# Attention in a transformer layer: row tile 0 is read and exponentiated behind tile 3, and ScalarE mixes row tile 2's far blocks ahead of q's evacuation

## The chip, the cores and the metric

The kernel runs on one core of a Trainium2 chip. The metric is device time in microseconds (us) of one execution, lower is better. Engines are named as in the profile: PE is the matrix engine (TensorE), DVE is VectorE, ACT is ScalarE, POOL is GpSimd, SP is the engine that issues most DMAs.

## The reference, cut to what matters

The input x is (8, 512, 512) in float32; there are 16 heads of 128. The layer is x + attention(layernorm(x)), then a routed feed-forward part on the result that the change does not touch. The attention mixes three softmaxes over the same scores:

```python
q = _rope((x @ Wq).reshape(b, n, H, HD)); k = _rope((x @ Wk).reshape(b, n, H, HD)); v = (x @ Wv).reshape(b, n, H, HD)
p_cmp = softmax over the 8 block means of k (blocks of 64 that lie fully in the past)
imp = p_cmp + 2.0 * cur_blk; sel = top_k(imp, 8)        # there are 8 blocks, so all are selected
p_slc = softmax(where(slc_mask, s_full, -1e30))         # the causal row
p_swa = softmax(where(causal & (i - j <= 64), s_full, -1e30))   # the window of 64
o = o_cmp * g_cmp + o_slc * g_slc + o_swa * g_swa
return o.reshape(b, n, H * HD) @ Wo
```

## The kernel before, in words

Matrix products are made of three passes over split operands (`hi` and `lo` parts), so each product needs a `hi` copy (ACT) and a `lo` difference (POOL or DVE) of its operands.

The attention is a software pipeline over 128 units. A unit is one head of one batch. In iteration u the engines work on three units at once: q, k and values of unit u are projected, unit u-1 is scored, and unit u-2 (in the code's numbering for the parts called `end`) has its probabilities transposed and multiplied with the values. A unit's 512 query rows are four row tiles t of 128 rows; tile t has its scores in PSUM bank t, and because of causality only the first (t+1)*128 columns count. Bank 0 has room left beside the 128 columns of tile 0, and there `sc` lies (the compressed branch's block sums of all four tiles, L428).

Nothing schedules this at run time: each engine has its own in-order program, written out by hand in a function `body` per engine, and semaphores tie them together.

- **PE** (L668): projects q and then k (24 matmuls, L650), scores the four tiles in the order 0, 3, 2, 1 (12 matmuls, L693), transposes the probabilities (10, L707), projects the values (24, L663), multiplies with the values (12, L728). The scores wait for `lo_done` of q and k from POOL, and tile by tile for `probs_ready` from DVE.
- **ACT** (L812): in one iteration it copies the finished output (`output_out`, L795), evacuates q from PSUM (`evacuate(u, 0)`, L764), mixes the far blocks of tiles 2 and 1 into `probs` (`mix_far`, L801: three instructions for tile 2, one for tile 1), copies the values (L809), evacuates k (L764 again), makes the `hi` parts of the transposed probabilities (L776), and then the exponentials of the rows (L782) and windows (L788) of tile 3, the `hi` copy of q (L771), the exponentials of tiles 2 and 1, the compressed branch's exponential (L843), the exponentials of tile 0, and the `hi` copy of k (L771). In the iterations that prepare the next pair of heads' weights, and in the last pair with those of Wo, it also makes weight copies (L152, L156, L1088), mostly behind the `hi` copy of k.
- **SP** (L524): stores the output, then moves the two halves of the evacuated q (later k) across partitions into `s_swap` (L501, L502), as the rotation of rope needs.
- **POOL** (L610): for q and then k three operations of rope each (L600, L601, L604), then the two `lo` parts (L608). The first waits for the evacuation and for the swap's landing.
- **DVE** (L936): causal mask (L897) of tiles 3 and 0; `read` of tile 3, which is the row minimum (L888), the window's minimum (L890) and the block sums into `sc` (L892); the `lo` parts of the transposed probabilities (L902); the mask of tiles 2 and 1; `read` of tiles 2, 1 and 0; the compressed branch (L954 to L960), which waits at L966 for ACT's exponentials; the coefficients, with `cmp_step` 7 at L972; then the mixes (L910, L926), of which the near part of tile 2 waits for ACT's far part (L985).

`masked_at` gives each tile's place in the list `MASKED`, the order of DVE's reads, and ACT's exponentials wait by it (L780, L787). ACT's evacuation of q waits for PE's projection of q and for POOL's `lo` of the q before it, since both use `s_full`:

```python
act.wait_ge(projected[k], u + 1)
act.wait_ge(lo_done[k], u)
nc.scalar.activation(s_full[k][:], banks[QK_BANK[k]][:, :], ACT.Copy, ...).then_inc(evacuated[k], 1)
```

Of the kernel before, what the change touches and what calls it, by code (L numbers as in the profile page):

```python
# [17 lines left out]
T = N // P  # L18
# [378 lines left out]
def attend(nc, phase, banks, m, gates, gates_full, xt_hi, xt_lo, weights, rope_d, misc_d, o_dram, gates_dram, chunks):  # L397
# [46 lines left out]
    cmp_step, exp_cmp, exp_row, exp_win = S("cmp_step"), S("exp_cmp"), S("exp_row"), S("exp_win")  # L444
# [13 lines left out]
    def pt_bank(u, g):  # L458

        if isinstance(u, int) and u >= U:  # L460
            return banks[((6, 5, 7), (0, 1, 2))[u - U][g]]
        return banks[(6, 5, 4)[g]]

    def out_bank(u):

        return banks[0 if isinstance(u, int) and u == U + 1 else 6]

    SCORED = [0, 3, 2, 1]
    MASKED = [3, 2, 1, 0]
    MIXED = [0, 3, 2, 1]  # L470
    scored_at = {t: i + 1 for i, t in enumerate(SCORED)}
    masked_at = {t: i + 1 for i, t in enumerate(MASKED)}
    mixed_at = {t: i + 1 for i, t in enumerate(MIXED)}
# [3 lines left out]
    def near(t):  # L477

        lo = WIN if t == 0 else 0
        return lo, t * P - WIN + lo, (t + 1) * P  # L480
# [277 lines left out]
    def scalar(act):  # L758
        def evacuate(u, k):

            act.wait_ge(projected[k], u + 1)
            if not (isinstance(u, int) and u == 0):
                act.wait_ge(lo_done[k], u)
            nc.scalar.activation(s_full[k][:], banks[QK_BANK[k]][:, :], ACT.Copy, scale=(-HD ** -0.5 if k == 0 else 1.0))\  # L764
                .then_inc(evacuated[k], 1)

        def high(u, k):
            act.wait_ge(roped[k], u + 1)
            if not (isinstance(u, int) and u == 0):
                act.wait_ge(scores_ready, u * T)  # L770
            nc.scalar.activation(qk_hi[k][:], s_full[k][:], ACT.Copy).then_inc(hi_done[k], 1)  # L771

        def pt_high(u, g):
            w = (512, 384, 384)[g]
            act.wait_ge(pt_ready, (u - 2) * 3 + g + 1)
            nc.scalar.activation(pt_hi[:, PTOFF[g]:PTOFF[g] + w], pt_bank(u, g)[:, 0:w], ACT.Copy).then_inc(pt_hi_done, 1)  # L776

        def exp_of_row(u, t):

            act.wait_ge(row_read, (u - 1) * T + masked_at[t])  # L780
            n = banks[t][:, 0:(t + 1) * P]
            nc.scalar.activation(n, n, ACT.Exp, bias=shift1[:, t:t + 1], scale=-1.0,  # L782
                                 accum_out=sums[:, 1, t:t + 1]).then_inc(exp_row, 1)

        def exp_of_window(u, t):
            lo = near(t)[0]
            act.wait_ge(win_masked, (u - 1) * T + masked_at[t])  # L787
            nc.scalar.activation(win[:, t, lo:], win[:, t, lo:], ACT.Exp, bias=shift2[:, t:t + 1], scale=-1.0,  # L788
                                 accum_out=sums[:, 2, t:t + 1]).then_inc(exp_win, 1)

        def output_out(u):

            act.wait_ge(out_ready, u - 2)
            act.wait_ge(out_slot_free, (u - 3) * 16 + 16)
            nc.scalar.activation(o_sb[:], out_bank(u - 1)[:, :], ACT.Copy).then_inc(out_evacuated, 1)  # L795

        def mix_far(v, t):

            act.wait_ge(cmp_step, v * NC + 7)
            for b in range(near(t)[1] // BS):  # L800
                last = nc.scalar.activation(probs[:, E1OFF[t] + b * BS:E1OFF[t] + (b + 1) * BS], banks[t][:, b * BS:(b + 1) * BS],  # L801
                                            ACT.Identity, scale=coef[:, 1, t:t + 1], bias=cb[:, t, b:b + 1])
            last.then_inc(far_mixed, 1)

        def values_high(u, j):

            act.wait_ge(projected[2], u)
            a, b = value_slots((j - 1) % 4)
            nc.scalar.activation(v_hi[:, a:b + 1:b - a].rearrange("p a i d -> p a (i d)"),  # L809
                                 banks[7][:, :].rearrange("p (a n) -> p a n", a=2), ACT.Copy).then_inc(v_hi_done, 1)  # L810

        def body(p, k, j, project=True, score=True, end=True, values=True, output=True, split=False, first=False):  # L812
            u = unit(p, k, j)
            if output:
                output_out(u)
            if project:
                evacuate(u, 0)
            if end:
                mix_far(u - 2, 2)
                mix_far(u - 2, 1)  # L820
            if values:
                values_high(u, j)
            if project:
                evacuate(u, 1)
            if first is not False:
                chunks.high_first(act, first)
            if end:
                for g in range(3):
                    pt_high(u, g)
            if score:  # L830
                exp_of_row(u, 3)
                exp_of_window(u, 3)
            if project:
                high(u, 0)
            if split is not False:
                weights.high(act, split, 0, j % 2)
            if score:
                exp_of_row(u, 2)
                exp_of_window(u, 2)
                exp_of_row(u, 1)  # L840
                exp_of_window(u, 1)
                act.wait_ge(cmp_step, (u - 1) * NC + 3)
                nc.scalar.activation(sc, sc, ACT.Exp).then_inc(exp_cmp, 1)  # L843
                exp_of_row(u, 0)
                exp_of_window(u, 0)
            if project:
                high(u, 1)
            if split is not False:
                if j % 2:
                    act.wait_ge(projected[2], split * PAIR)  # L850
                    weights.high_v(act, split)
                weights.high(act, split, 1, j % 2)

        def quad(p, k, split=False, wo=(), o=False):
            for j in range(4):
                body(p, k, j, split=split if j >= 2 else False)
                if j in wo:
                    chunks.high_wo(act, wo[j])
                if o and j < 2:
                    chunks.high_half(act, 2 * j)  # L860

        nc.scalar.activation(gates_full[:], gates_full[:], ACT.Sigmoid).then_inc(gates_squashed, 1)
        body(0, 0, 0, score=False, end=False, values=False, output=False)
        body(0, 0, 1, end=False, output=False)
        act.wait_ge(gates_stored, 16)
        body(0, 0, 2, output=False)
        body(0, 0, 3)
        for k in range(1, 3):
            quad(0, k)
        for p in range(1, PAIRS):  # L870
            quad(p - 1, 3, split=p)
            for k in range(0, 3):
                quad(p, k, wo=({}, {0: 0, 1: 1, 2: 2, 3: 3}, {0: 4, 1: 5, 2: 6, 3: 7})[k] if p == PAIRS - 1 else {})
        quad(PAIRS - 1, 3, wo={2: 8, 3: 9}, o=True)
        body(PAIRS, 0, 0, project=False, first=1)
        for n in range(10, H):
            chunks.high_wo(act, n)
        body(PAIRS, 0, 1, project=False, score=False, values=False, first=2)
        output_out(U + 2)
        chunks.high_first(act, 3)  # L880

    def vector(dve):
        def read(v, t):

            nb = 2 * (t + 1)
            n = banks[t]
            dve.wait_ge(causal_masked, v * T + MASKED_AT[t])
            nc.vector.tensor_reduce(shift1[:, t:t + 1], n[:, 0:(t + 1) * P], AX.X, ALU.min)  # L888
            lo, k0, k1 = near(t)
            nc.vector.tensor_tensor_reduce(out=win[:, t, lo:], in0=n[:, k0:k1], in1=m("window")[:, lo:], scale=1.0, scalar=3e38,  # L890
                                           op0=ALU.add, op1=ALU.min, accum_out=shift2[:, t:t + 1]).then_inc(win_masked, 1)
            nc.vector.reduce_sum(sc[:, t, 0:nb], n[:, 0:nb * BS].rearrange("p (n s) -> p n s", s=BS), AX.X).then_inc(row_read, 1)  # L892

        def mask(v, t):
# [19 lines left out]
        def mix_far(t):  # L914
            if t:
                k0 = near(t)[1]
                mix(t, (0, k0 // BS), probs[:, E1OFF[t]:E1OFF[t] + k0])
# [18 lines left out]
        def body(p, k, j, project=True, score=True, end=True, split=False):  # L936
            u = unit(p, k, j)
            v = u - 1
            gate = gates[:, bass.ds(k * 4 + j, 1)].rearrange("p o (r t) -> p (o r) t", t=T)
            if score:  # L940

                mask(v, 3)
                mask(v, 0)
                read(v, 3)
            if end:
                for g in range(3):
                    pt_low(u, g)
            if score:
                mask(v, 2)
                mask(v, 1)  # L950
                for t in (2, 1, 0):
                    read(v, t)
                dve.wait_ge(row_read, v * T + T)
                nc.vector.scalar_tensor_tensor(out=sc, in0=sc, scalar=-1.0 / BS,  # L954
# [820 lines left out]
```

## Time and profile before

| what | value |
|---|---|
| median of 3 runs | 2373.87 us (2372.65 to 2376.27) |
| the profiled execution's own time | 2379.06 us |
| its span, first to last instruction | 2377.1 us |
| mean granted TensorE clock | 0.994 of full speed |
| PE busy | 2309.4 us, 97% of the span |
| PE weight loads busy | 2031.2 us, 85% |
| DVE busy | 1844.1 us, 78% |
| POOL busy | 1633.4 us, 69% |
| ACT busy | 1489.1 us, 63% |

Busy time is a share of the whole span, which has several stages; the attention takes it from about 70 us to about 1800 us. The chain that ended last is PE for 66% of the span, DVE 11%, POOL 9%, ACT 5%, DMA 3%.

### The profile page before, as it was taken

What the parts mean: (1) busy time and instruction counts of PE and PEld (TensorE: products, weight loads), DVE (VectorE), ACT (ScalarE), POOL (GpSimd) and SP (SyncE); (2) the same over time, 40 slices, a digit from 0 to 9 for tenths busy, and PEclk for the clock granted to TensorE, in tenths of its full rate; (3) what the DMA queues carried; (4) which work ended last, traced back from release to release, by engine and by line L of the source; (5) the groups of instructions that cost most, each with busy time, mean ns of one, the idle gap of its engine ahead of it and who ended that gap; (6) DMA issues with size and microseconds to landing.
All of it is one profiled execution on the core that took longest, in us unless ns stands there. A gap on an engine that the chain in (4) does not pass through costs nothing.

```text
span 2377.1 us, 42098 instructions
## 1 busy us (share of the span) xinstructions
PE 2309.4 (97%) x13200; PEld 2031.2 (85%) x13200; DVE 1844.1 (78%) x6091; ACT 1489.1 (63%) x4174; POOL 1633.4 (69%) x1273
## 2 busy tenths in 40 slices
PE   6899999999999999999999999999998999998998
PEld 5799899988988998999899898888887788886787
DVE  8589898988988898898989898888884665566511
ACT  6577777777777777777777777777773111113343
POOL 2677877787777778777877877787883444444554
PEclk9999999999999999999999999999999999999999
DMA  5222222222222222222222222223333444453332
GB/s 173 74 58 64 73 76 54 72 78 63 59 72 78 54 67 82 64 58 76 74 63 59 73 76 54 71 83 93 85 89 123 167 170 153 152 196 105 110 117 80
DMA packets 143601, 213.34 MB, mean 90 GB/s; under 512 B 15008, under 2 KB 53280, under 8 KB 143392
## 3 DMA queue, kind: packets, MB, share of 16 engines
q1 hardware_dynamic: 137248, 196.17, 28.1%
q10 hardware_dynamic: 4224, 8.39, 0.9%
q0 software_dynamic: 1920, 6.24, 0.8%
q8 instruction: 101, 1.65, 0.3%
q14 instruction: 108, 0.88, 0.1%
HBM read 90.47 MB, written 53.22 MB: 60 GB/s over the span
## 4 chain that ended last, share of the span: by engine, by line
PE 66%; DVE 11%; POOL 9%; ACT 5%; DMA 3%; issue 2%; SPq 0%; POOLq 0%; ACTq 0%; DVEq 0%
PE bank L650 19%; PE bank L1132 13%; PE bank L663 10%; PE bank L693 7%; PE bank L728 7%; PE bank L707 4%; DMA s_swap<-s_full 3%; PE bank L1693 3%; PE bank L1674 3%; POOL s_full L600 3%; POOL s_swap L601 3%; POOL s_full L604 3%; DVE bank L892 1%; DVE pt_lo L902 1%; DVE shift L888 1%
## 5 line engine op out<-in xcount | busy, mean ns | idle before, releaser
L600 POOL TENSOR_TENSOR s_full<-s_full,rope 128x512 f32<-128x512 f32 x256 | 334.2, 1305 | 328.6 <-DMA s_swap<-s_full 328.3
L604 POOL TENSOR_TENSOR s_full<-s_full,s_swap 128x512 f32<-128x512 f32 x256 | 330.9, 1292 | 37.6 <-POOL s_swap L601 0.9
L601 POOL TENSOR_TENSOR s_swap<-s_swap,rope 128x512 f32<-128x512 f32 x256 | 330.9, 1293 | 0.0
L608 POOL TENSOR_TENSOR qk_lo<-s_full,qk_hi 128x512 fp32r<-128x512 f32 x256 | 326.3, 1294 | 0.0
L776 ACT ACTIVATE pt_hi<-bank 128x384 fp32r<-128x384 f32 (+1 forms) x384 | 174.4, 528 | 226.1 <-PE bank L707 226.1
L663 PE MATMUL bank<-wv_hi,xt_hi 128*128 128x256 f32 x1024 | 300.3, 293 | 0.0
L782 ACT ACTIVATE bank<-bank,shift 128x512 f32<-128x512 f32 (+3 forms) x512 | 257.1, 502 | 57.7 <-DVE bank L892 57.4
L663 PE MATMUL bank<-wv_hi,xt_lo 128*128 128x256 f32 x1024 | 290.0, 283 | 0.0
L663 PE MATMUL bank<-wv_lo,xt_hi 128*128 128x256 f32 x1024 | 289.9, 283 | 0.0
L1113 POOL TENSOR_TENSOR o_lo<-o_raw,o_hi 128x2048 fp32r<-128x2048 f32 x31 | 144.3, 4654 | 212.0 <-ACT o_hi L1292 185.5
L892 DVE TENSOR_REDUCE bank<-bank 128x8 f32<-128x512 f32 (+3 forms) x512 | 253.1, 494 | 0.0
L888 DVE TENSOR_REDUCE shift<-bank 128x1 f32<-128x512 f32 (+3 forms) x512 | 246.2, 481 | 0.0
L910 DVE SCALAR_TENSOR_TENSOR bank<-bank,coef,cb 128x192 f32<-128x192 f32 (+1 forms) x512 | 195.4, 405 | 55.0 <-ACT probs L801 55.0
L788 ACT ACTIVATE win<-win,shift 128x192 f32<-128x192 f32 (+1 forms) x512 | 225.6, 441 | 0.0
L771 ACT ACTIVATE qk_hi<-s_full 128x512 fp32r<-128x512 f32 x256 | 161.4, 630 | 91.1 <-POOL s_full L604 86.9
L902 DVE TENSOR_TENSOR pt_lo<-bank,pt_hi 128x384 fp32r<-128x384 f32 (+1 forms) x384 | 206.9, 594 | 8.4 <-ACT pt_hi L776 8.4
L650 PE MATMUL bank<-xt_hi,wq_hi 128*128 128x512 f32 x512 | 207.9, 406 | 0.8 <-PEq L201 0.8
L1132 PE MATMUL bank<-wo_hi,o_hi 128*128 128x512 f32 x512 | 205.2, 401 | 1.7 <-ACT s_swap L795 1.6
L650 PE MATMUL bank<-xt_hi,wq_lo 128*128 128x512 f32 x512 | 200.4, 391 | 0.0
L1132 PE MATMUL bank<-wo_hi,o_lo 128*128 128x512 f32 x512 | 200.4, 391 | 0.0
L1132 PE MATMUL bank<-wo_lo,o_hi 128*128 128x512 f32 x512 | 200.0, 391 | 0.0
L650 PE MATMUL bank<-xt_hi,wk_hi 128*128 128x512 f32 x512 | 199.2, 389 | 0.0
(190 smaller groups left out, 6899.1 us busy)
## 6 DMA issues: line engine op xcount, KB each, us to landing
s_swap<-s_full SPq DMA_DIRECT2D x512, 128.0 KB, 2.3
o_scratch<-s_swap SPq DMA_DIRECT2D x128, 256.0 KB, 2.0
o_raw<-o_scratch SPq DMA_DIRECT2D x32, 1024.0 KB, 5.4
w_raw<-in_L_ffn_W SPq DMA_DIRECT2D x64, 256.0 KB, 2.9
xin<-in_L_attn_x SPq DMA_DIRECT2D x14, 1024.0 KB, 5.5
z_scratch<-z ACTq DMA_DIRECT2D x8, 1024.0 KB, 4.3
out<-x SPq DMA_DIRECT2D x32, 256.0 KB, 2.1
wq_raw<-in_L_attn_Wq SPq DMA_DIRECT2D x16, 256.0 KB, 3.0
```

The costliest lines, as they stand in the source:

```text
L600: nc.gpsimd.tensor_tensor(s_full[k][:], s_full[k][:], rope[:, 0, :], ALU.mult).then_inc(cos_done[k], 1)
L601: nc.gpsimd.tensor_tensor(s_swap[k][:], s_swap[k][:], rope[:, 1, :], ALU.mult).then_inc(sin_done[k], 1)
L604: nc.gpsimd.tensor_tensor(s_full[k][:], s_full[k][:], s_swap[k][:], ALU.add).then_inc(roped[k], 1)
L608: nc.gpsimd.tensor_tensor(qk_lo[k][:], s_full[k][:], f32(qk_hi[k][:]), ALU.subtract).then_inc(lo_done[k], 1)
L650: last = nc.tensor.matmul(banks[QK_BANK[k]][:, :], w[k][s][:, c, :], v[:, b, c, :], start=(n == 0), stop=(n == 3 * C - 1))
L663: last = nc.tensor.matmul(out, x[:, b, c, at:at + P], w[:, c, :], start=(n == 0), stop=(n == 3 * C - 1), skip_group_check=True)
L782: nc.scalar.activation(n, n, ACT.Exp, bias=shift1[:, t:t + 1], scale=-1.0, accum_out=sums[:, 1, t:t + 1]).then_inc(exp_row, 1)
L788: nc.scalar.activation(win[:, t, lo:], win[:, t, lo:], ACT.Exp, bias=shift2[:, t:t + 1], scale=-1.0, accum_out=sums[:, 2, t:t + 1]).then_i ...
L888: nc.vector.tensor_reduce(shift1[:, t:t + 1], n[:, 0:(t + 1) * P], AX.X, ALU.min)
L892: nc.vector.reduce_sum(sc[:, t, 0:nb], n[:, 0:nb * BS].rearrange("p (n s) -> p n s", s=BS), AX.X).then_inc(row_read, 1)
L902: nc.vector.tensor_tensor(pt_lo[:, PTOFF[g]:PTOFF[g] + w], pt_bank(u, g)[:, 0:w], f32(pt_hi[:, PTOFF[g]:PTOFF[g] + w]), ALU.subtract).then ...
L1132: last = self.nc.tensor.matmul(self.bank(b, t)[:, :], o[k % 2][:, g, t * P:(t + 1) * P], w[:, k * self.G + g, :], start=(k == 0 and n == 0 ...
```

## The change

The order in which DVE reads the tiles becomes 3, 0, 2, 1; its read of tile 0 moves from behind tile 1 to directly behind tile 3, ahead of the `lo` parts of the probabilities. ACT's exponentials of tile 0 (row and window) move to directly behind those of tile 3, ahead of the `hi` copy of q. The exponential of tile 1's window moves behind the compressed branch's exponential. ACT's three mixing instructions for tile 2 move from behind the evacuation of q to ahead of it. DVE gets a new wait ahead of the block sums of tiles 2 and 1: `sc` is in bank 0, where ACT now works on tile 0's exponential at about that time.

```diff
-    MASKED = [3, 2, 1, 0]
+    MASKED = [3, 0, 2, 1]
...
             if output:
                 output_out(u)
+            if end:
+                mix_far(u - 2, 2)
             if project:
                 evacuate(u, 0)
             if end:
-                mix_far(u - 2, 2)
                 mix_far(u - 2, 1)
...
             if score:
                 exp_of_row(u, 3)
                 exp_of_window(u, 3)
+                exp_of_row(u, 0)
+                exp_of_window(u, 0)
             if project:
                 high(u, 0)
...
                 exp_of_row(u, 1)
-                exp_of_window(u, 1)
                 act.wait_ge(cmp_step, (u - 1) * NC + 3)
                 nc.scalar.activation(sc, sc, ACT.Exp).then_inc(exp_cmp, 1)
-                exp_of_row(u, 0)
-                exp_of_window(u, 0)
+                exp_of_window(u, 1)
...
+            if masked_at[t] > masked_at[0]:
+                dve.wait_ge(exp_row, v * T + masked_at[0])
             nc.vector.reduce_sum(sc[:, t, 0:nb], ...).then_inc(row_read, 1)
...
                 read(v, 3)
+                read(v, 0)
...
-                for t in (2, 1, 0):
+                for t in (2, 1):
                     read(v, t)
```

## Rows read from the trace of the kernel before

**Rows 1.** Busy us by stretch (PE, PEld, DVE, ACT, POOL; clock, DMA share, GB/s).

```profile
1000.00:1100.00 100.00, 100.00 (x615) 90.53 (x614) 89.39 (x322) 75.48 (x232) 77.22 (x61) 1.00 0.22 59
```

**Rows 2.** The chain in order of time: start us, duration us, what.

```profile
1002.71 5.52 PE bank L650 x24
...
1015.96 5.52 PE bank L650 x24
```

**Rows 3.** Who waited for whom, whole kernel: us in total, times, longest.

```profile
DVE sums L966 <- ACT bank L782: 99.3, 128, 2.3
...
PEld bank L693 <- DVE probs L926: 18.1, 26, 1.6
```

**Rows 4.** ACT's timeline in one unit: start us, duration us, instruction.

```profile
1004.33 0.63 ACT L771 ACTIVATE qk_hi<-s_full 128x512 fp32r<-128x512 f32 x1
1004.85 0.59 ACT L795 ACTIVATE s_swap<-bank 128x512 f32<-128x512 f32 x1
1005.54 0.60 ACT L764 ACTIVATE s_full<-bank 128x512 f32<-128x512 f32 x1
1006.03 1.28 ACT L801 ACTIVATE probs<-bank,cb,coef 128x64 f32<-128x64 f32 x4
1007.19 0.62 ACT L809 ACTIVATE v_hi<-bank 128x512 fp32r<-128x512 f32 x1
```

**Rows 5.** POOL's timeline for the same unit (in brackets: idle before, releaser).

```profile
1009.18 1.29 POOL L600 TENSOR_TENSOR s_full<-s_full,rope 128x512 f32<-128x512 f32 x1 [2.75 <-DMA s_swap<-s_full]
...
1015.79 1.29 POOL L604 TENSOR_TENSOR s_full<-s_full,s_swap 128x512 f32<-128x512 f32 x1
1017.04 2.54 POOL L608 TENSOR_TENSOR qk_lo<-s_full,qk_hi 128x512 fp32r<-128x512 f32 x2
```

**Rows 6.** ACT's and POOL's timeline in a stretch that follows a late transfer.

```profile
832.79 0.60 ACT L764 ACTIVATE s_full<-bank 128x512 f32<-128x512 f32 x1
845.62 0.60 ACT L764 ACTIVATE s_full<-bank 128x512 f32<-128x512 f32 x1
...
844.23 2.54 POOL L608 TENSOR_TENSOR qk_lo<-s_full,qk_hi 128x512 fp32r<-128x512 f32 x2
```

**Rows 7.** ACT's timeline at the change of weight pair, units 30 and 31.

```profile
482.60 0.59 ACT L795 ACTIVATE s_swap<-bank 128x512 f32<-128x512 f32 x1
483.08 0.60 ACT L764 ACTIVATE s_full<-bank 128x512 f32<-128x512 f32 x1
...
495.81 1.05 ACT L156 ACTIVATE wv_hi<-wv_raw 128x1024 fp32r<-128x1024 f32 x1
496.76 0.62 ACT L152 ACTIVATE wk_hi<-wk_raw 128x512 fp32r<-128x512 f32 x1
```

**Rows 8.** The chain in order of time, transfers of q's and k's halves.

```profile
564.36 3.95 DMA s_swap<-s_full
...
1433.76 2.37 DMA s_swap<-s_full
...
1664.40 3.81 DMA s_swap<-s_full
```

**Rows 9.** PE's timeline: first matmul of iteration 3, of iteration 127, first score.

```profile
107.62 0.45 PE L650 MATMUL bank<-xt_hi,wq_hi 128*128 128x512 f32 x1
...
1767.75 0.45 PE L650 MATMUL bank<-xt_hi,wq_hi 128*128 128x512 f32 x1
...
1021.32 0.22 PE L693 MATMUL bank<-qk_hi,qk_hi 128*128 128x128 f32 x1
```

**Rows 10.** DVE's timeline around the reads, one unit.

```profile
1013.92 0.56 DVE L892 TENSOR_REDUCE bank<-bank 128x6 f32<-128x384 f32 x1
...
1017.43 0.19 DVE L966 TENSOR_REDUCE sums<-bank 128x4 f32<-128x32 f32 x1 [0.71 <-ACT bank L782]
```

**Rows 11.** ACT's timeline of the exponentials, same unit (tile 3's window, tile 0's row).

```profile
1012.51 0.47 ACT L788 ACTIVATE win<-win,shift 128x192 f32<-128x192 f32 x1
...
1016.85 0.34 ACT L782 ACTIVATE bank<-bank,shift 128x128 f32<-128x128 f32 x1
```

## The prediction

> **What bounds the kernel now.** I read the busy shares by stretch first. In the middle of the attention PE is busy for 100 of 100 us at full clock; DVE has 89, POOL 77, ACT 75 [rows 1]. The chain in order of time then gives the rhythm: the projection of q and k starts at 1002.71 and again at 1015.96, so a unit takes 13.25 us, and every piece between is PE [rows 2]. From the first matmul of iteration 3 (107.62) to that of iteration 127 (1767.75) pass 1660.1 us for 124 units, 13.39 each [rows 9]; 124 times 13.25 is 1643. So all of PE's stalls in the attention are worth about 17 us, and no reordering of other engines can win more than that there by much. Who-waited-for-whom names what the change aims at: DVE waits for ACT's last exponential 128 times, 99.3 us, and PE's weight loads wait for DVE's mixes, 18.1 us [rows 3].
>
> What the averages hide is a second loop that is almost as long as PE's. Evacuation of q (ACT) leads to the swap (DMA), to six rope operations (POOL), to the `hi` copy of k (ACT), to the output copy, to the next evacuation of q. All of it is serial: ACT's program is in order, and one `s_full` and one `s_swap` serve each of q and k. In one unit: evacuation starts at 1005.54 [rows 4], POOL starts on it at 1009.18, so 3.64; its last rope operation ends at 1015.79 + 1.29 = 1017.08, so 7.90 [rows 5]. Where PE is not the limit, after a late transfer, the evacuations stand at 832.79 and 845.62, 12.83 apart, the second just behind the first half of POOL's `lo` pair, which began at 844.23 and takes 2.54 for two [rows 6]. So the loop's free length is 12.83, and it has 13.25 - 12.83 = 0.42 of cover under PE.
>
> **The change part by part.**
>
> *Tile 2's far mixes ahead of q's evacuation.* Nothing is added, three instructions are moved, but into the loop. Four take 1.28 with the last one's full length in it, and the next instruction starts at 1007.19, 1.16 after the first: a slot of 0.29 each, 0.87 for three [rows 4]. ACT's own way round is 3.64 + 7.90, a hop from POOL to ACT, the `hi` copy's slot of 0.52 (1004.33 to 1004.85) [rows 4], and the output copy's slot of 0.48 (482.60 to 483.08) [rows 7]. No row shows the hop alone; it is at least 0 and at most the 845.62 - 845.50 = 0.12 from the end of POOL's first `lo` to the evacuation [rows 6]; I take 0.06, the middle. That makes 12.60 before, hidden under POOL's 12.83, and 12.60 + 0.87 = 13.47 after. POOL cannot hide it: its route to the evacuation ends with the `lo` of q, 1.27 behind the last rope operation, and ACT's now takes 0.06 + 0.52 + 0.48 + 0.87 = 1.93. The loop becomes longer than PE's 13.25 by 0.22, over 124 units 27 us. All that the evacuation issues goes with it: the two swaps on SP's queue come 0.87 later against the output's store, which only gives the store more room, and POOL, which has 2.75 idle before its first rope operation [rows 5], starts later. Late next is POOL's `lo` of k: it ends at 1017.04 + 2.54 = 1019.58 and PE's first score needs it at 1021.32 [rows 5, 9]. The evacuation drifts by 0.22 a unit until these 1.7 us are gone, within about 8 units, and from then on PE waits there in every unit. mix_far's own wait, for DVE's coefficients, is met: DVE is tied to PE's time, while ACT's turn drifts away from it.
>
> *What the cover absorbed until now.* A loop that is the bound absorbs nothing. (a) Late transfers: the chain has 12 swaps of 3.15 to 4.18 us, the first at 564.36 and the last at 1664.40, against a usual 2.37; together 18 us over it [rows 8]. Now all 18 count. (b) Weight pairs: at each of 7 changes ACT copies one more 512-column operand behind the `hi` copy of k in one unit (0.52, the slot of such a copy in rows 4), and 0.95 + 0.52 in the next (495.81 to 496.76 and one more such slot) [rows 7]: 2.0 each, 14 us. (c) The last pair's copies for the output projection stand in the same place: 9 of 0.52 and two of twice the width at 0.95, 6.6 us, an estimate from the same slots. (d) Jitter of the loop's members: 0.05 a unit, 6 us, an estimate; rope operations last 1.29 but now and then more.
>
> *Tile 0's read and exponentials moved.* DVE's work is the same, and the read phase ends at the same time; the `lo` parts come some 0.75 later, and PE uses them only after 24 value matmuls. Gain: at L966 DVE waits 0.71 for tile 0's row [rows 10], which now is long done; left is the wait for the compressed exponential, so about 0.45 is won. But DVE is not what PE waits for once the loop is the bound. Worth 0 then; without the loop it would be part of the 18 us.
>
> *The new wait on DVE.* Queued behind it are the block sums of tiles 2 and 1 and all that follows. DVE reaches the first at 1013.92 [rows 10], 0.75 later after the move, 1014.7. ACT does tile 0's row behind tile 3's window, which started at 1012.51, so by about 1013.4 (its slot and the 0.34 of a 128-column exponential) [rows 11]. Margin 1.2; cost 0. If ACT were late by more, each tenth would cost PE at most a tenth.
>
> *A rule against the trace.* PE is busy 100% of this stretch, its weight loads 90% [rows 1], and yet my sum is made of a loop in which PE has no part. The Trainium skill (Perfetto Trace Analysis, Identifying the Most-Contended Engine) says that kernels improve through the engine with the highest occupancy, though for TensorE it wants weight loads, not matmul time, as the measure. By that rule an edit on ACT and DVE is worth 0, not 55 us.
>
> **The sum.** 124 x 13.47 = 1670.3, plus 6, 18, 14 and 6.6, is 1715 against 1660: 55 us more. The profiled execution took 2379.06, its span 2377.1; it becomes 2434. The median of the runs is 5 lower, 2373.87, so 2429.
>
> **The rivals.**
> 1. *The gain comes through*: the evacuation has room after all, for instance because the slots overlap better, and PE's waits for DVE's mixes go: 18.1 us [rows 3], 2356. It needs a loop below 13.25, that is 0.22 less than the rows give; the rows' spread is a third of this. 4%.
> 2. *Nothing moves*, because PE covers all: 2374. The same condition, with the gain lost to the pair changes. The page's rule above would end here. 3%.
> 3. *The new DVE wait decides* together with the loop: it does so if ACT finishes tile 0's row later than 1014.7, 1.2 us later than worked out. A late swap does it, since tile 2's exponential stands behind the `hi` copy of q; at 0.2 a unit more, 25 us on top, 2454. For it speaks that ACT is in order; against it the margin. 8%.
> 4. *The change does not do what it says*: far mixes that wait for DVE's coefficients would hold the evacuation even longer. In the rows the coefficients are ready at about the output copy; this would end in the range of case 3. Counted there.
>
> The forecast itself has 85%.
>
> **How the numbers follow.** Down: the hop at 0 (7 us), only 5 late transfers (10), the copies for weights partly beside a wait (10) give 2402. Up: slower rope operations by 0.1 (12 us), 18 late transfers (9), and part of case 3 give 2458. Runs of this kernel tell 0.2%, 5 us, from no change. Faster by more than that 4%, within it 3%, slower 93%.
>
> **What would show it.** Right: evacuations of q 13.4 to 13.5 apart in the middle, where they were 13.25; in PE's waits a new entry of some 0.2 us for POOL's `lo` of k before the first score, 100 times or more; the chain running through ACT, DMA and POOL instead of PE; PE's share of the attention down by 2 to 3 points; DVE's wait at L966 halved. Wrong: a unit still at 13.25, or PE waiting for DVE's mixes instead of POOL's `lo`; a unit of 13.7 or more would mean the new wait or the coefficients hold ACT.

## The result, and the profile after

| | median | runs |
|---|---|---|
| before | 2373.48 us | 5 (2371.25 to 2376.27) |
| changed | 2417.83 us | 5 (2416.8 to 2420.8) |

The ratio is 1.0185, with a 95% interval of 1.0173 to 1.0198: slower by 44 us. The forecast was 2429 (2402 to 2458), that is 55 us more, and slower with 93%. The profiled execution of the changed kernel has a span of 2414.9 us, 37.8 more than before.

The same stretch by busy shares (columns as in [rows 1]):

```profile
1000.00:1100.00 100.00, 99.71 (x615) 88.09 (x615) 87.65 (x310) 71.83 (x221) 73.25 (x58) 1.00 0.24 62
```

Busy time all but hides the loss. PE was 100.00 and is 99.71, since the ends of matmuls are modelled in this profile and hide small holes; the weight loads (90.53, now 88.09) tell more, and so does the number of instructions of POOL, 58 in place of 61. ACT does the same work and is idler. The chain that ended last, by engine, says it plainly (it was PE 66%, POOL 9%, ACT 5%, DMA 3%):

```profile
POOL 40%; PE 20%; DMA 13%; ACT 11%; issue 7%; DVE 3%; SPq 3%; POOLq 0%; ACTq 0%; DVEq 0%
```

The chain in order of time shows the loop that I had worked out from [rows 4 to 6], link by link, for one unit (start, duration, what; short issue pieces left out):

```profile
1013.98 2.37 DMA s_swap<-s_full
...
1016.48 1.30 POOL s_full L600
1017.78 1.27 POOL s_swap L601
...
1019.18 1.29 POOL s_full L604
1020.47 1.24 POOL s_full L600
1021.72 1.26 POOL s_swap L601
...
1023.11 1.30 POOL s_full L604
...
1024.97 0.58 ACT s_swap L795
1025.55 0.15 ACT probs L801
...
1025.73 0.70 ACT probs L801 x2
1026.44 0.50 ACT s_full L764
...
1027.45 2.39 DMA s_swap<-s_full
```

1013.98 to 1027.45 is 13.47. ACT's timeline of the same unit has the moved instructions between the output's copy and the evacuation, and ACT now waits for POOL ahead of the `hi` copy of k, which it did not in [rows 4]:

```profile
1024.43 0.63 ACT L771 ACTIVATE qk_hi<-s_full 128x512 fp32r<-128x512 f32 x1 [1.09 <-POOL s_full L604]
1024.97 0.58 ACT L795 ACTIVATE s_swap<-bank 128x512 f32<-128x512 f32 x1
1025.45 0.99 ACT L801 ACTIVATE probs<-bank,cb,coef 128x64 f32<-128x64 f32 x3
1026.31 0.61 ACT L764 ACTIVATE s_full<-bank 128x512 f32<-128x512 f32 x1
```

And DVE and PE, in who-waited-for-whom (us in total, times, longest):

```profile
DVE bank L913 <- ACT probs L801: 162.1, 251, 2.2
...
PEld bank L693 <- issue: 55.7, 127, 3.5
PEld bank L693 <- DVE probs L929: 47.2, 125, 1.7
```

PE waits twice in every unit at the scores. The profile names no releaser for the first wait, but it ends when POOL's pair of `lo` parts does: the pair that starts at 1010.87 and takes 2.55 ends at 1013.42, and the first weight load of the scores starts at 1013.49. In all 127 units with this wait the distance is 0.07 to 0.11 us:

```profile
1013.49 0.19 PEld L693 LDWEIGHTS bank<-qk_hi,qk_hi 128*128 128x128 f32 x1 [0.33 <-issue]
...
1014.56 0.19 PEld L693 LDWEIGHTS bank<-qk_hi,qk_hi 128*128 128x128 f32 x1 [0.22 <-DVE probs L929]
```

The second is for DVE's mix, and DVE is late there because tile 1's far mix stands behind the evacuation, which has drifted; DVE's near mix of tile 1 waits for it, and the window mix that PE needs comes after:

```profile
1013.77 0.43 DVE L913 SCALAR_TENSOR_TENSOR bank<-bank,coef,cb 128x192 f32<-128x192 f32 x1 [0.36 <-ACT probs L801]
```

So PE's wait for DVE, which had been 18.1 us [rows 3], is 47.2; with tile 1's far mix ahead of the evacuation too (the kernel with four, below) it is 14.3. The two waits add up to 103 us, while the iterations of the changed kernel are only 56.6 us over 13.25 each: a weight load that waits is not a PE that waits, microsecond for microsecond.

I split the attention by PE's first projection matmul of each iteration and took 13.25 off every unit. What is left over, in us ("around" takes iterations 15 to 17, 31 to 33 and so on):

| units | before | changed |
|---|---|---|
| around the 7 changes of weight pair (3 units each) | 8.6 | 21.8 |
| last pair | 4.2 | 10.0 |
| all others but the first four | 4.3 | 24.8 |

The difference is 39.5 us from iteration 3 to iteration 127; with the first units it is 39.0, and iteration 127 begins at 1806.71 in place of 1767.75 [rows 9]. The profiled execution before was 5 us above the median of its kernel, so this pair shows less than the 44 us of the medians; the second pair of profiles (experiments 9 and 10) has 42.1 us over the same iterations.

### The profile page after: what moved, and what is told of

The parts are those of the page before. It is cut to its first block, busy times and chain, and to the rows that moved or that the text cites. A ratio compares the mean times of both kernels' runs of the same rounds, so it can differ in the third digit from the quotient of the medians.

```text
span 2414.9 us, 42099 instructions
## 1 busy us (share of the span) xinstructions
PE 2333.6 (97%) x13200; PEld 2011.9 (83%) x13200; DVE 1843.1 (76%) x6091; ACT 1477.4 (61%) x4174; POOL 1630.4 (68%) x1273
## 4 chain that ended last, share of the span: by engine, by line
POOL 40%; PE 20%; DMA 13%; ACT 11%; issue 7%; DVE 3%; SPq 3%; POOLq 0%; ACTq 0%; DVEq 0%
POOL s_full L600 13%; POOL s_swap L601 13%; PE bank L1136 13%; POOL s_full L604 13%; DMA s_swap<-s_full 13%; ACT probs L801 5%; PE bank L1697 3%; PE bank L1678 3%; ACT s_swap L795 3%; ACT s_full L764 3%; SPq L501 2%; DVE junk L1457 0%; ACT wo_hi L1092 0%; ACT wk_hi L152 0%; PE bank L1374 0%
## 5 line engine op out<-in xcount | busy, mean ns | idle before, releaser
L913 DVE SCALAR_TENSOR_TENSOR bank<-bank,coef,cb 128x192 f32<-128x192 f32 (+1 forms) x512 | 208.1, 407 | 162.5 <-ACT probs L801 162.1
L693 PE MATMUL bank<-qk_hi,qk_hi 128*128 128x128 f32 (+3 forms) x512 | 181.7, 355 | 31.8 <-DVE probs L929 14.9
```

Source lines behind the costliest of these rows:

```text
L913: return nc.vector.scalar_tensor_tensor(out=to.rearrange("p (n s) -> p n s", s=BS), in0=e, scalar=coef[:, 1, t:t + 1], in1=cb[:, t, b0:b1] ...
```

## The experiments

There are eleven runs: eight edits, and three kernels once more. Each is compared with the kernel before on the same chip (its median was 2375 to 2376 us there).

**1. The far mixes alone.** On the kernel before:

```diff
+            if end:
+                mix_far(u - 2, 2)
             if project:
                 evacuate(u, 0)
             if end:
-                mix_far(u - 2, 2)
                 mix_far(u - 2, 1)
```

> The kernel before with one edit: tile 2's three far mixes ahead of q's evacuation; tile 0 stays where it was. My theory (the evacuation loop of ACT, DMA and POOL became 13.47 us long, over PE's 13.25): evacuations of q 13.47 apart, 2413 to 2422 us, the whole loss of the change. Rival (the tile 0 part with DVE's new wait carries the loss): 2374, units of 13.25. Halfway, 2395, would mean that both parts carry.

Measured: 2420.11 us, ratio 1.0181 (1.0164 to 1.0198). Evacuations 13.49 apart in the median. The whole loss is in the three moved instructions.

**2. Tile 0 alone.** The changed kernel with that edit undone; the new wait on DVE stays.

> The changed kernel with the far mixes put back behind q's evacuation: only tile 0's earlier read and exponentials and DVE's new wait are left. My theory: the loop is 12.83 to 12.87 again and hidden under PE; units of 13.25, 2368 to 2376 us. Rival (the new wait decides): 2400 or more, and DVE idle ahead of the block sums of tile 2.

Measured: 2365.81 us, ratio 0.9955 (0.9938 to 0.9972): faster than both kernels, and 2 us below my range. Who-waited-for-whom of this kernel:

```profile
DVE sums L969 <- ACT bank L844: 40.6, 128, 0.9
...
PEld bank L693 <- DVE probs L928: 10.3, 22, 1.3
```

DVE's wait for the exponentials went from 99.3 to 40.6 us, PE's for the mixes from 18.1 to 10.3 [rows 3]. DVE has no wait ahead of the block sums of tiles 2 and 1 in this trace, nor in the changed kernel's. The left-over above 13.25 is 4.8 us around the pair changes in place of 8.6, 1.3 in the last pair in place of 4.2, 2.5 elsewhere in place of 4.3. ACT's timeline shows a link that I had left out:

```profile
1001.05 0.18 ACT L844 ACTIVATE bank<-bank 128x32 f32<-128x32 f32 x1
1001.15 0.45 ACT L788 ACTIVATE win<-win,shift 128x192 f32<-128x192 f32 x1
...
1001.59 0.62 ACT L771 ACTIVATE qk_hi<-s_full 128x512 fp32r<-128x512 f32 x1
```

From the compressed exponential to the `hi` copy of k pass 0.54. Before, the row and the window of tile 0 with their accumulator reads stood between, in place of one window, and it took 0.82:

```profile
1003.51 0.18 ACT L843 ACTIVATE bank<-bank 128x32 f32<-128x32 f32 x1 [0.24 <-DVE bank L960]
```

That is the time to the `hi` copy of k at 1004.33 [rows 4]. K's rope was done at 1003.93 in that unit (a rope operation ends 13.2 us ahead of the 1017.08 of [rows 5]), so the copy stood ready 0.4 us before ACT came to it. In quiet units PE covers that; where a unit has more to do on ACT it does not, and there the profile shows what it is worth. At the changes of weight pair in iterations 16 and 80 no swap was late in either kernel (POOL's start over 4.2 us behind the evacuation); these iterations were 0.90 and 0.92 us over 13.25 before and are 0.34 and 0.32 here. In iteration 16 PE loses its time in one wait, for DVE's mixes (the kernel before, then this one):

```profile
287.35 0.19 PEld L693 LDWEIGHTS bank<-qk_hi,qk_hi 128*128 128x128 f32 x1 [1.07 <-DVE probs L926]
```

```profile
286.44 0.19 PEld L693 LDWEIGHTS bank<-qk_hi,qk_hi 128*128 128x128 f32 x1 [0.49 <-DVE probs L928]
```

In the kernel before the chain leads back from it through DVE's near mix and ACT's far mixes, evacuation of q, output copy and weight copies to the compressed exponential, and not through the swap and POOL. That exponential starts 1.42 us behind the iteration's first matmul before and 1.14 here, which goes with DVE's shorter wait for the exponentials, and the `hi` copy of k follows it by 0.53 in place of 0.83. So about half of this gain comes by way of DVE and half by way of ACT. Seven changes at 0.58 are 4 us of the 9 to 10. Much of the rest lies in units behind late swaps, of which the two profiles of before have 13 and 10 and the two of this kernel 6 and 3; how much of it is tile 0's doing is not shown.

**3 to 5. The dose.** The changed kernel with one, two and four far mixes ahead of the evacuation (three is the change):

```diff
             if end:
-                mix_far(u - 2, 2)
+                mix_far(u - 2, 2, 0, 1)      # or 0, 2
             if project:
                 evacuate(u, 0)
             if end:
+                mix_far(u - 2, 2, 1)         # or 2
                 mix_far(u - 2, 1)
```

For four, `mix_far(u - 2, 1)` goes ahead of the evacuation with the three.

> The changed kernel with only the first of tile 2's three far mixes ahead of q's evacuation. ACT's way round the loop is then 12.60 + 0.29 = 12.89, about POOL's 12.83. My theory: a threshold; under 13.25 the loop costs nothing in quiet units, so 2368 to 2380 us. Rival (each instruction ahead of the evacuation costs its slot, 0.29 x 124 = 36 us for all three, 12 each): 2386.

> The changed kernel with two of tile 2's three far mixes ahead of q's evacuation. ACT's way round is 12.60 + 0.58 = 13.18, just under PE's 13.25. My theory: quiet units still 13.25, but almost no cover is left, so weight pairs and late transfers cost nearly in full: 2385 to 2400 us. Rival (in proportion, two thirds of 44 us): 2403.

> The changed kernel with tile 1's far mix ahead of q's evacuation too, four in all. My theory: the loop is the bound, so each slot more counts in full: units of 13.76, 0.29 x 126 = 37 us above the changed kernel, 2450 to 2458 us. Rival (PE is bound by DVE's mixes, which come sooner by this): 2418 or less.

| ahead of the evacuation | ACT's way round, worked out | evacuations apart, median | time | ratio (95%) |
|---|---|---|---|---|
| 0 | 12.60 | 13.26 | 2365.81 | 0.9955 (0.9938 to 0.9972) |
| 1 | 12.89 | 13.26 | 2368.08 | 0.9966 (0.9954 to 0.9979) |
| 2 | 13.18 | 13.18 | 2380.85 | 1.0019 (1.0008 to 1.0029) |
| 3 | 13.47 | 13.49 | 2417.83 | 1.0185 (1.0173 to 1.0198) |
| 4 | 13.76 | 13.79 | 2465.35 | 1.0372 (1.0355 to 1.0389) |

This is a threshold and no straight line: the first instruction costs 1 to 2 us, within the intervals, the second 13, the third 37, the fourth 48. With two, the quiet unit still has room, but after each disturbance it wins back only 0.07 in place of 0.42; PE's own work on a unit takes 13.25, so a median of 13.18 between evacuations means that most units are still catching up (78 of 121 distances are under 13.22). I had put this kernel at 2385 to 2400 us, 4 us too high at least: disturbances did not cost nearly in full. The fourth missed my 37 and my range by 7 us: its way round is as worked out, but late swaps took 21.6 us there and 4.9 in the changed kernel (below), a difference larger than the 11 us that my 37 lacks; how much of it counts no run separates.

**6. The output's copy behind the evacuation**, in the changed kernel, to take another 0.48 out of the loop:

```diff
-            if output:
-                output_out(u)
             if end:
                 mix_far(u - 2, 2)
             if project:
                 evacuate(u, 0)
+            if output:
+                output_out(u)
...
-            if output:
-                store(p, k, j)
             if project:
                 swap(u, 0)
+            if output:
+                store(p, k, j)
```

> The changed kernel with the output's copy moved from ahead of q's evacuation to behind it, and the store behind q's swap on SP's queue. This takes 0.48 out of the loop: 13.47 - 0.48 = 12.99, under PE's 13.25. My theory: units of 13.25 again, 2362 to 2378 us. Rival (what slows is something else than the loop's length, the new wait or DVE's mixes): 2418 stays.

Measured: 2380.64 us, ratio 1.0021 (1.0012 to 1.0031). By the ratios 39 of the 44 us are gone: the loop's length it was, though the time lies 2.6 us above my range. The evacuations came out 13.13 apart in the median and not under PE's cover at 12.99. The store is now issued on the heels of q's swap, and POOL's start follows the evacuation by 3.76 in the median in place of 3.65, which is most of it (for one unit):

```profile
1008.01 0.60 ACT L764 ACTIVATE s_full<-bank 128x512 f32<-128x512 f32 x1
1008.49 0.61 ACT L795 ACTIVATE s_swap<-bank 128x512 f32<-128x512 f32 x1
```

```profile
1011.81 1.27 POOL L600 TENSOR_TENSOR s_full<-s_full,rope 128x512 f32<-128x512 f32 x1 [2.73 <-DMA s_swap<-s_full]
```

**7. The same edit in the kernel before**, with the output's copy behind tile 2's far mixes.

> The kernel before with the same edit: the output's copy behind q's evacuation and tile 2's far mixes. POOL's way round (12.83) was the longer one there, so theory: no change in quiet units and little elsewhere, 2366 to 2378 us. If the ACT way were what limits after late transfers, the free unit would go from 12.83 to about 12.4.

Measured: 2404.27 us, ratio 1.0120 (1.0101 to 1.0138). A clear miss: 29 us slower than before, and the free unit was no shorter (12.94 at least). The output's copy uses the buffer into which k is swapped (`s_swap[1]`), so k's swap waits on SP until the store has landed. SP's timeline and POOL's in one such unit:

```profile
736.51 0.36 SPq L512 DMA_DIRECT2D o_scratch<-s_swap  x1
740.31 0.46 SPq L501 DMA_DIRECT2D s_swap<-s_full  x1
```

```profile
743.27 1.29 POOL L600 TENSOR_TENSOR s_full<-s_full,rope 128x512 f32<-128x512 f32 x1 [1.03 <-DMA s_swap<-s_full]
```

POOL, in the middle of its work, waits for k, which it did for 4 us in all before and does for 20 here. The left-over around the pair changes is 24.9 us. Experiment 6 has the copy 0.9 us sooner after the evacuation, and that wait is 6.7 us in all. That the late store is the cause of all 29 us is argued from these waits; no run separates it.

**8. One transfer in place of two.** In the changed kernel:

```diff
+            if k == 0:
+                sp.dma_start(s_swap[k][:, :], s_full[k][:, :]).then_inc(swapped[k], 16)
+                return
             sp.dma_start(s_swap[k][0:64, :], s_full[k][64:128, :]).then_inc(swapped[k], 16)
             sp.dma_start(s_swap[k][64:128, :], s_full[k][0:64, :]).then_inc(swapped[k], 16)
```

> The changed kernel with q's two half swaps (0.51 us of issue between them) replaced by one DMA of 128 partitions that does not swap the halves; q's rope is computed from the wrong halves, and all else is done. It takes the second issue out of the loop: the evacuation to POOL's start goes from 3.64 to 3.1 or 3.4 (twice the bytes in one transfer). My theory: loop 12.95 to 13.25, so units of 13.25, 2370 to 2385 us. Rival (the DMA is hidden anyway): 2418.

Measured: 2367.45 us, ratio 0.9965 (0.9953 to 0.9977), 3 us below my range. POOL's start is 3.05 behind the evacuation (1002.61 to 1005.66):

```profile
1005.66 1.29 POOL L603 TENSOR_TENSOR s_full<-s_full,rope 128x512 f32<-128x512 f32 x1 [2.46 <-DMA s_swap<-s_full]
```

0.6 us out of a link that is easily passed over, an issue on SP, brings back all 44 us, with the far mixes left where the change put them. It bounds what a faster swap could bring; as a kernel it is of no use.

**9 to 11. Once more**: the kernel before, the changed one, and tile 0's part alone.

> The kernel before, once more, for its profile alone: 13 swaps of q were late there (evacuation to POOL's start over 4.2 us), 6 in the changed kernel. If the number belongs to the kernel, 11 or more here, in units near 37 to 55 and 101 to 119; if it belongs to the execution, anything from 5 to 16.

> The changed kernel, once more, for its profile alone. If the number of late swaps belongs to the kernel, 4 to 8 and worth about 5 us, in units 46, 63, 92, 98, 104, 121; if it belongs to the execution, up to 16. Units of 13.47 in either case.

> Only tile 0's part of the change, timed in more rounds. It measured 0.9955 of the time of before; theory (ACT reaches the hi copy of k 0.4 us sooner, which shortens the loop at weight pairs and in the last pair): 0.994 to 0.998 again. Rival (the first measurement was a lucky draw of late transfers): 0.998 to 1.002.

Measured: 2375.0 us with 10 late swaps, all but one of them in units from 37 to 55 and 101 to 113; 2417.61 with 5, each in a unit of the first run's list; and 2367.01, ratio 0.9963 (0.9950 to 0.9975). The gain of tile 0's part is there again. On the late swaps the answer is mixed: the changed kernel was as expected, but 10 is short of the 11 that I had asked for if the number belongs to the kernel, and the two profiles of tile 0's part have 6 and 3, with one unit in common. The same kernel tends to be hit in the same units; how often differs from run to run.

## Why the prediction was right, and which terms were off

**The loop** is as the first part had it. Worked out 13.47, measured 13.47 in the unit above and 13.49 in the median. The members are those of the rows: 3.65 to POOL's start, 7.92 of rope, the hop 0.03 (I took 0.06 from between 0 and 0.12), slots of 0.54, 0.48 and 0.86. Experiments 1, 3 to 6 and 8 shorten or lengthen it by different members and the time follows. PE's wait at the first score came as described, but from iteration 3 on and not after a drift of some 8 units. DVE's wait for the exponentials halved as I had said (99.3 to 47.2 us). PE's busy share of the attention did not fall by 2 to 3 points: it went from 99.2% to 98.5%, and only the weight loads, from 89.5% to 86.4%, fell by that much. PE waiting for DVE's mixes stood among my signs of being wrong, in place of the wait for `lo`; it came beside it, in every unit.

**Weight pairs and the last pair** were put at 14 + 6.6 us; the ACT links of these units took 20.2 us more than 1.93 each (0.51 and 1.46 at each change). The term holds.

**Late transfers** were the mis-sized term. I wrote "Now all 18 count", and took for granted that as many swaps would be late as before. 13 were late before, worth 19 us over 3.63 each, and 6 in the changed kernel, worth 5; with 5 in place of 18 the sum would have been 42 and not 55. The iterations 3 to 127, for which the sum was made, grew by 39.5 and 42.1 us in the two pairs of profiles, and the medians of the runs by 44. That the far mixes alone had 11 late swaps, worth 11.6 us, in a loop of the same length, shows how the term can vary; these iterations were 5.6 us longer there. What goes with a late swap is in the transfers' queues, for 0.8 us of the first late unit before (q evacuated at 563.23, landed at 568.3):

```profile
q1 hardware_dynamic: 91, 0.16, 88.9%
q8 instruction: 1, 0.02, 10.9%
```

One packet of 16 KB of instructions moves among the swap's packets; which of the 16 DMA engines carried it the trace does not say. Each of the 12 swaps that were late by over 1 us had such a packet begin 2.4 to 2.6 us after the evacuation, while the second half was moving. In the changed kernel the packet of most of these units begins 3.1 to 3.8 us after it, when the swap is almost home. Over all twelve traces with q's swap in two halves, such a packet began 1.2 to 3.05 us after the evacuation in 77 units, and POOL's start was late in all 77. It is not the only cause: units 63 and 121 of the changed kernel were late with no such packet. So whether a fetch hits seems to be a matter of phase between the program and the loop, which an edit that shifts the loop can change; that is argued, and no run tests it. With four mixes ahead 16 swaps were late, for 21.6 us. What sets the moment of a fetch I did not find out.

**Tile 0** I called worth 0 beside the longer loop, and without the loop a part of the 18 us. Both hold in the number: far mixes alone take 2420, the whole change 2418, and alone it is worth 9 to 10 us. The 0.45 us that DVE was to win at its wait measured 0.46 (99.3 less 40.6, over 128 units). The reason was half wrong: I costed the edit on DVE only, not the 0.28 us that it takes away between the compressed exponential and the `hi` copy of k on ACT; and "DVE is not what PE waits for once the loop is the bound" fails as a statement, since PE waits 47.2 us for DVE's mixes in the changed kernel, in 125 units, held up there by the loop itself. From tile 0's part alone to the whole change it is 52 us, from 2365.8 to 2417.8: the longer loop costs its own length and swallows this gain.

**The new wait** cost 0, as worked out. **The rule of the page** (the Trainium skill, Perfetto Trace Analysis, Identifying the Most-Contended Engine) would have given 0. PE had the highest occupancy before and has it after, 97% of the span both times, so by this trace the rule does not price an edit on another engine; the advice of the Trainium skill (Perfetto Trace Analysis, Optimization Strategy), to find what blocks the full engine at its gaps by its semaphores, is the one that this case bears out: PE's gap at 1013.49 ends 0.07 us behind POOL's `lo`, for which its program waits. Before the change it would have shown nothing in a quiet unit, where PE had no gap.

## What to carry to other kernels

When one engine is full, look for the second-longest loop: follow one buffer from its evacuation through every engine until it is evacuated again, and compare the sum with the period. Cover under the bound, here 0.42 us, is what a move may spend; the first instructions moved are free and the next ones cost their whole slot in every round. And price the two halves of a change apart, because one may carry a gain that the other swallows: tile 0's part alone, 2366 to 2367 us, is the version to keep.

## What the runs showed of the hardware that was not expected

A single 16 KB packet of instructions that begins 1.2 to 3.05 us after the evacuation of q went with a late swap in 77 of 77 units; a transfer of 128 KB then landed up to 1.8 us late (4.18 in place of 2.37). It tends to hit the same units of the program from run to run (5 of 6 in the changed kernel). After one transfer of 256 KB over 128 partitions POOL could start 0.6 us sooner (3.05 in place of 3.65) than after two of 128 KB issued one behind the other.
